# Graph network kernel: layer 0 multiplies h by the neighbour weights before it takes neighbour means

## The reference

```python
h = relu(layernorm(x))
mask = (adj > 0)
deg = sum(mask, axis=1)
agg = mask @ h / max(deg, 1)
self_f = h @ W_self + b_self
nb_f = agg @ W_nb + b_nb
x = x + relu(concatenate([self_f, nb_f]) @ W_comb + b_comb)
h = relu(layernorm(x))
# layer 1: five steps of a gated propagation with adj and adj.T, then two dense layers
x = x + layer1(h, adj)
```

## Time and profile before

| | us |
|---|---|
| median of 3 runs | 1231.34 (1231.26 to 1233.05) |
| profiled execution, its own time | 1229.56 |
| its span, first to last instruction | 1227.8 |
| TensorE busy | 1218.7 (99%) |
| VectorE busy | 757.1 (62%) |
| ScalarE busy | 287.8 (23%) |

### The profile page before, as it was taken

How to read it: one execution, slowest core, us unless ns; L and a number is a source line. 1 busy time by engine, 2 the same in 40 slices (tenths; PEclk the granted TensorE clock), 3 DMA queues, 4 the chain that set the end, 5 groups by cost and what they waited for, 6 DMA issues and landing times.

```text
span 1227.8 us, 12867 instructions
## 1 busy us (share of the span) xinstructions
PE 1218.7 (99%) x4872; PEld 589.9 (48%) x4872; DVE 757.1 (62%) x1264; ACT 287.8 (23%) x568; POOL 15.4 (1%) x15
## 2 busy tenths in 40 slices
PE   8999999999999999999999999999999999999998
PEld 5766644444444444444444444444444444444445
DVE  6677735787984474487367339626725864662674
ACT  5766100022321121033012113301202230120121
POOL 4000000000000000000000000000000000000000
PEclk9999999999999999999999999999999999999999
DMA  9545734960019505800830660191084039015202
GB/s 330 172 155 172 291 138 172 315 240 0 1 34 341 207 0 179 300 1 35 311 135 0 243 236 1 57 352 71 3 307 169 1 141 336 2 69 206 90 1 69
DMA packets 44506, 180.61 MB, mean 147 GB/s; under 512 B 3489, under 2 KB 13474, under 8 KB 29346
## 3 DMA queue, kind: packets, MB, share of 16 engines
q1 hardware_dynamic: 43440, 176.04, 39.5%
q0 software_dynamic: 720, 3.67, 0.8%
q10 hardware_dynamic: 290, 0.14, 0.0%
HBM read 144.71 MB, written 35.13 MB: 146 GB/s over the span
## 4 chain that ended last, share of the span: by engine, by line
PE 93%; DVE 4%; DMA 1%; issue 1%; ACT 1%; SPq 0%; DVEq 0%
PE bank L352 90%; PE bank L418 1%; PE bank L520 1%; DMA SN<-in_x 1%; PE bank L439 0%; ACT A L770 0%; PE bank L470 0%; DVE LF L1203 0%; PE bank L380 0%; DVE stat L993 0%; DVE GR L1350 0%; DVE first_GZ L1350 0%; DVE first_GH L1323 0%; DVE first_GZ L1353 0%; DVE GR L1353 0%
## 5 line engine op out<-in xcount | busy, mean ns | idle before, releaser
L352 PE MATMUL bank<-slot,LF 128*128 128x512 f16 x1792 | 389.4, 379 | 0.0
L352 PEld LDWEIGHTS bank<-slot,LF 128*128 128x128 f16 x1792 | 175.3, 98 | 210.1 <-issue 2.3
L352 PE MATMUL bank<-X,W 128*128 128x512 f32 x384 | 180.5, 592 | 0.0
L352 PE MATMUL bank<-XT,W 128*128 128x512 f32 x288 | 135.3, 592 | 0.0
L352 PEld LDWEIGHTS bank<-X,W 128*128 128x128 f32 x384 | 72.5, 190 | 88.0 <-issue 86.9
L352 PE MATMUL bank<-AT,SN 128*128 (+1 forms) x256 | 97.0, 379 | 0.0
L352 PE MATMUL bank<-A,SN 128*128 (+1 forms) x256 | 97.0, 379 | 0.0
L1249 DVE TENSOR_TENSOR u_buf<-bank,m_buf 128x512 f32<-128x512 f32 x16 | 11.1, 692 | 134.0 <-PE bank L352 134.0
L352 PEld LDWEIGHTS bank<-XT,W 128*128 128x128 f32 x288 | 54.7, 190 | 68.9 <-issue 68.2
L770 ACT ACTIVATE m_buf<-bank 128x512 f32<-128x512 f32 x46 | 27.4, 595 | 231.9 <-PE bank L352 231.9
L352 PE MATMUL bank<-DR,work 128*128 128x512 f16 x256 | 65.6, 379 | 0.4 <-DVE DR L1064 0.2
(11 more groups left out here) (217 smaller groups left out, 1420.9 us busy)
## 6 DMA issues: line engine op xcount, KB each, us to landing
slot<-quad_d SPq DMA_DIRECT2D x112, 1024.0 KB, 4.9
WG<-in_adj SPq DMA_DIRECT2D x32, 512.0 KB, 4.4
quad_d<-AT SPq DMA_DIRECT2D x12, 1024.0 KB, 5.0
quad_d<-A SPq DMA_DIRECT2D x12, 1024.0 KB, 8.6
quad_d<-spare SPq DMA_DIRECT2D x4, 1024.0 KB, 4.0
SN<-in_x SPq DMA_DIRECT2D x2, 1024.0 KB, 10.3
x_d<-SN POOLq DMA_DIRECT2D x4, 512.0 KB, 4.2
x1o<-x_d SPq DMA_DIRECT2D x1, 2048.0 KB, 8.1
```

The source lines that it names most:

```text
L352: return pe.matmul(o, l, r, start=start, stop=stop, skip_group_check=again)
```

## The change

Since a mean over neighbours and a product with weights can be exchanged, h is multiplied by the neighbour slices of `W12` first (`values`), and the neighbour sums run over these values. `hi_lo` now holds two fp16 parts of the values and a column of ones. In `mean_sum` the mask tiles are stationary and the values move (256 columns, and 257 with the ones, which gives the degree), so sums come out with nodes on partitions, one tile in each of banks 0 to 3. The neighbour weights are scaled by a norm computed in the front (`w2_norm`). Own products (`own_term`) are made in bank 7 while a block's sums still run, DVE keeps them with the bias (`keep_own`), and `sums` combines straight from the banks. `values`, `turn_h`, `turn_h2` and `own_term` share bank 7. In the front, loads are cut and reordered, weight products and bias row come first, and values of the first quarter and the turns of two quarters are made before the loop; the 12 bias columns go one by one into the first 12 steps. At the end, the last two output tiles are added and stored singly, one of them issued by ACT.

```diff
-STAGE_AT = [8, 13, 14]
-H2_BANKS = [6, 6, 6, 4]
-H2_AT = 12
+STAGE_AT = [7, 12, 13]
 ACT_MOVES = [i for i in range(NT * NB) if i % 2 == 0 or (i >= NT and i % NT in (3, 11))]
-HIGH_AT = [1, 4, 8]
-LOW_AT = [2, 5, 9]
-TURN_AT = [4, 7, 10, 12]
+G_AT = {0: (1, 0), 1: (1, 1), 4: (2, 0), 5: (2, 1), 8: (3, 0), 9: (3, 1)}
+T_AT = {2: (2, 0), 3: (2, 1), 6: (3, 0), 7: (3, 1)}
+H2_AT = (10, 12)
+OWN_AT = 14
+COLUMNS = 300
...
+        hi_lo = at("hi_lo", 144 * KB, [P, NT, 2 * D + 2], FP16)
...
+        term = [own0[:, 0, :], own0[:, 1, :], h2[:, 2, :], h2[:, 3, :]]
...
+        low_banks = ctx.enter_context(nc.psum_tensor("low_banks", [P, 4, 512], FP32))
+        bank = [low_banks[:, i, :] for i in range(4)]
+        bank += [ctx.enter_context(nc.psum_tensor(f"bank{i}", [P, 512], FP32)) for i in range(4, 8)]
...
+        def value_bank(q, a):
+            return bank[4 + a] if q == 0 else bank[7]
...
+            sp.dma_start(wgR[0][:, 0, :], wg_t[0:P, :]).then_inc(ld_wj[0], 16)
+            sp.dma_start(ioR[:, 0, 0, :], w_in[0:P, :]).then_inc(ld_wj[0], 16)
+            x_quarter(0)
+            x_quarter(1)
+            sp.dma_start(wgR[0][:, 1, :], wg_t[P:2 * P, :]).then_inc(ld_wj[1], 16)
+            sp.dma_start(ioR[:, 0, 1, :], w_in[P:2 * P, :]).then_inc(ld_wj[1], 16)
+            sp.dma_start(wgR[1][:, 0, :], wg_t[2 * P:3 * P, :]).then_inc(ld_wo[0], 16)
+            sp.dma_start(ioR[:, 1, 0, :], w_out[0:P, :]).then_inc(ld_wo[0], 16)
+            x_quarter(2)
+            x_quarter(3)
+            sp.dma_start(wgR[1][:, 1, :], wg_t[3 * P:4 * P, :]).then_inc(ld_wo[1], 16)
+            sp.dma_start(ioR[:, 1, 1, :], w_out[P:2 * P, :]).then_inc(ld_wo[1], 16)
...
+            sp.wait_ge(o2_dve, 2 * NB - 1)
+            sp.dma_start(out_v[:, NT - 4:NT - 2, :], res[:, NT - 4:NT - 2, :]).then_inc(st_out, 16)
+            sp.wait_ge(o2_dve, 2 * NB + 1)
+            sp.dma_start(out_v[:, NT - 1, :], res[:, NT - 1, :]).then_inc(st_out, 16)
+            sp.wait_ge(st_out, 16 * (NB + 1))
+            sp.wait_ge(st_last, 16)
...
+            def turn_h(q, f):
+                pe.wait_ge(h_ready, q + 1)
+                if q == 0:
+                    pe.wait_ge(w12_out, 2)
+                if q == 1 and f == 0:
+                    pe.wait_ge(hT_act, 1)
+                if q == 1 and f == 1:
+                    pe.wait_ge(hT_dve, 1)
+                if q >= 2 and f == 0:
+                    pe.wait_ge(g_lo, 2 * q)
+                if q >= 2 and f == 1:
+                    pe.wait_ge(hT_act, q + 1)
+                o = bank[6 + f] if q < 2 else bank[7]
+                for t in range(BT):
+                    last = pe.transpose(o[:, t * P:t * P + P], h32[:, BT * q + t, f * P:f * P + P], ident)
+                last.then_inc(hT_ready, 1)
+            def values(q, a):
+                pe.wait_ge(hT_act, q + 1)
+                pe.wait_ge(hT_dve, q + 1)
+                pe.wait_ge(w2_ready, 1)
+                if q == 0 and a == 1:
+                    pe.wait_ge(bias_out, 1)
+                if q >= 1 and a == 1:
+                    pe.wait_ge(g_lo, 2 * q + 1)
+                o = bank[4 + a] if q == 0 else bank[7]
+                for e in range(2):
+                    n0 = q * BN + (2 * a + e) * P
+                    for f in range(FT):
+                        last = mm(o[:, e * D:e * D + D], ST[:, f, n0:n0 + P], W12[:, 2 + f, :], f == 0, f == 1)
+                last.then_inc(g_ready, 1)
...
+            for j in range(2):
+                pe.wait_ge(ld_wj[j], 32)
+                fuse(0, j)
+                fuse(1, j)
+                if j == 0:
+                    pe.wait_ge(w2_square, 1)
+                    mm(bank[4][:, 0:1], one_col, norm[:, 0:1], True, True).then_inc(w2_norm, 1)
+            turn_h(0, 0)
+            turn_h(0, 1)
+            pe.wait_ge(ld_wo[0], 32)
+            pe.wait_ge(fused_out, 2)
+            fuse(2, 0)
+            pe.wait_ge(fused_out, 4)
+            fuse(3, 0)
+            values(0, 0)
+            values(0, 1)
+            pe.wait_ge(ld_wo[1], 32)
+            fuse(2, 1)
+            fuse(3, 1)
+            turn_h(1, 0)
+            turn_h(1, 1)
...
+                for q in range(BT):
+                    if m == 0 and b > 0:
+                        pe.wait_ge(agg_read, BT * (b - 1) + q + 1)
+                    l = mk[:, q * P:q * P + P]
+                    if m == 0:
+                        mm(bank[q][:, 0:D + 1], l, hi_lo[:, m, D:2 * D + 1], True, False, True)
+                    last = mm(bank[q][:, 0:D], l, hi_lo[:, m, 0:D], False, False, True)
+                    if m > 0:
+                        last = mm(bank[q][:, 0:D + 1], l, hi_lo[:, m, D:2 * D + 1], False, m == NT - 1, True)
+                last.then_inc(mask_used, 1)
...
+            def own_term(b, half):
+                pe.wait_ge(hT_act, b + 1)
+                pe.wait_ge(hT_dve, b + 1)
+                if b == 0 and half == 0:
+                    pe.wait_ge(g_lo, 8)
+                elif b > 0 and half == 1:
+                    pe.wait_ge(s_dve, b)
+                else:
+                    pe.wait_ge(own_kept, 2 * b + half)
+                for e in range(2):
+                    n0 = b * BN + (2 * half + e) * P
                     for f in range(FT):
-                        mm(bank[f][:, :], hi_lo[:, m, s, f * P:f * P + P], mk, m == 0 and s == 0,
-                           m == NT - 1 and s == 1)
+                        last = mm(bank[7][:, e * D:e * D + D], ST[:, f, n0:n0 + P], W12[:, f, :], f == 0, f == 1)
+                last.then_inc(own_made, 1)
...
+                if i < 12:
+                    bias_column(i)
+                if i in G_AT:
+                    values(*G_AT[i])
+                if i in T_AT:
+                    turn_h(*T_AT[i])
+                if b > 0 and m in H2_AT:
+                    turn_h2(b - 1, H2_AT.index(m))
+                if i == 11:
+                    own_term(0, 0)
+                if m == OWN_AT:
+                    own_term(b, 1)
                 if i + LEAD < NT * NB:
                     turn_adj(i + LEAD)
-                if i % NT == NT - 1:
-                    dense(i // NT, 0)
-                if i % NT == 1 and i > NT:
-                    dense(i // NT - 1, 1)
+                if m == NT - 1 and b + 1 < NB:
+                    own_term(b + 1, 0)
...
-            pe.wait_ge(agg_act, NB)
-            pe.wait_ge(agg_dve, NB)
-            pe.wait_ge(rdeg_ready, NB)
+            pe.wait_ge(agg_read, BT * NB)
...
-            dense(NB - 1, 1)
...
+            fused(0)
+            fused(1)
+            move_h(0)
+            convert(0, 0)
+            convert(0, 1)
+            high(0, 0)
+            convert(1, 0)
+            high(0, 1)
+            convert(1, 1)
+            act.wait_ge(var_ready, 2)
+            nc.scalar.activation(nrm[:, 1, 8:16], nrm[:, 0, 8:16], ACT.Sqrt).then_inc(sqrt_ready, 1)
+            fused(2)
+            fused(3)
+            move_h(1)
...
+            def low(q, a):
+                dve.wait_ge(g_hi, 2 * q + a + 1)
+                t = BT * q + 2 * a
+                v.tensor_tensor(hi_lo[:, t:t + 2, D:2 * D], value_bank(q, a)[:, :].rearrange("p (e d) -> p e d", e=2),
+                                hi_lo[:, t:t + 2, 0:D], ALU.subtract).then_inc(g_lo, 1)
...
+            dve.wait_ge(w2_norm, 1)
+            v.tensor_scalar(norm[:, 1:2], bank[4][:, 0:1], 1e-30, None, ALU.max).then_inc(w2_norm, 1)
+            variance(range(0, 8), 0)
+            dve.wait_ge(bias_made, 1)
+            v.tensor_copy(bias0, bank[5][:, 0:D]).then_inc(bias_out, 1)
+            newton(0, 8, 1)
             normal(0)
+            dve.wait_ge(w2_root, 1)
+            link(v.reciprocal(norm[:, 0:1], norm[:, 2:3]))
+            link(v.tensor_scalar(norm[:, 3:4], norm[:, 0:1], SCALE, None, ALU.mult))
+            v.tensor_scalar(w2, w2, norm[:, 3:4], None, ALU.mult).then_inc(w2_ready, 1)
+            turned_h(0)
             normal(1)
-            low(0)
+            dve.wait_ge(ld_x[2], 16)
+            row_stats(range(8, 12), 0)
+            low(0, 0)
+            dve.wait_ge(ld_x[3], 16)
+            row_stats(range(12, 16), 0)
+            low(0, 1)
+            variance(range(8, 16), 0)
+            turned_h(1)
+            newton(8, 16, 2)
+            normal(2)
...
+            def keep_own(b, half):
+                dve.wait_ge(own_made, 2 * b + half + 1)
+                dve.wait_ge(bias_out, 1)
+                if b > 0 and half == 1:
+                    dve.wait_ge(sn_hi, b)
+                for e in range(2):
+                    ins = v.tensor_tensor(term[2 * half + e], bank[7][:, e * D:e * D + D], bias0, ALU.add)
+                ins.then_inc(own_kept, 1)
...
+                link(v.tensor_scalar(rdeg[:, tiles], low_banks[:, :, D], 1.0, norm[:, 3:4], ALU.max, ALU.mult))
                 link(v.reciprocal(rdeg[:, tiles], rdeg[:, tiles]))
+                dve.wait_ge(own_kept, 2 * b + 2)
+                if b == 0:
```

(56 more changed lines are left out.)

336 lines of the change are left out of this document (131 added, 205 removed).

## The result

The changed kernel takes 1239.57 us (median; 1236.59 to 1244.95) against 1231.31 (1230.72 to 1233.05) on the same chip. The ratio is 1.0067, 95% interval 1.0054 to 1.0079: 8.3 us slower, where 2.9 were forecast, and outside the range. Its profiled execution took 1240.02 (span 1238.2), 10.4 more than that of before.

| us | before | after | difference | forecast |
|---|---|---|---|---|
| start to first neighbour sum | 27.67 | 39.40 | +11.7 | +5.1 |
| loop, to where spreading begins (before: its effective end) | 111.3 | 111.5 | +0.2 | -0.8 |
| spreading to the last matmul's end (before without the 3.46 of dense) | 1084.7 | 1084.7 | 0 | 0 |
| from there to the end | 4.1 | 2.6 | -1.5 | -1.4 |

The account below looks back on a forecast made before the run. TensorE was taken to bound the kernel, with 93% of the chain that ends last. Front +5.1, loop -0.8 and tail -1.4 gave +2.9 on 1231.3, so 1234.2 us; range 1226.5 to 1238.0.

Parts of the forecast that it names:

- Part 1: TensorE's work: one-column matmuls go, 512-column ones become twice as many of 256 or 257; net -5.7 us.
- Part 2: Front before the loop: first neighbour sum at 32.8 us against 27.67, so +5.1.
- Rival D: Before the first neighbour sum, 28.4 to 32.8: clock falls to 1.2 GHz, costing 2.2 us; total 1236.4, chance 10%.
- Part 3: Block 0, from first neighbour sum to node tile 14's transposes: 36.3 us, including 1.35 of stalls for the values' bank.
- Part 4: Blocks 1 to 3: TensorE stalls 1.9 us a block for VectorE's chain; block period 23.8 us.
- Rival B: Blocks 1 to 3: VectorE keeps up, stalls stay 0.6 us a block, period 22.5; total 1230.3, chance 22%.
- Part 5: End of the loop: TensorE stalls 2.3 us ahead of spreading; loop 110.5 us against 111.3.
- Part 6: Tail: smaller last addition and last transfer; -1.4 us, bounds 0 and -2.
- bound of +6.5 for the front: Front before the loop: upper bound on its added time, in us, if the weights land 1 us later.

Follow-up runs that it names:

- six mendings: Changed kernel with fusions reordered, GpSimd's second group held, 13 warm-up matmuls, two more ScalarE moves, ScalarE/VectorE front steps reordered, spreading bank by bank: 1228.69 us, ratio 0.9980.
- the changed order: Changed kernel with the first half of the output weights' fusions ahead of the first turn of h: 1237.48 us, ratio 1.0051.

## Why the prediction was right or wrong

**Part 1, TensorE's work: right.** A tile of sums alone takes 0.885 us (80.97 to 81.86), 0.874 were worked out from the straight line; over 64 tiles that is 0.7 us. An operation of 256 columns costs 0.885 / 8 = 111 ns, not 109, and the doubled number of weight loads cost nothing that shows. The net saving was 5.0 instead of 5.7.

**Part 2, the front: wrong, and it is nearly the whole miss.** First sum at 39.40 against 32.8; term by term:

| step of the walk | forecast | measured | miss |
|---|---|---|---|
| first product starts | 6.14 | 6.93 | +0.8 |
| weight products and bias row | 5.96 | 7.61 | +1.65 |
| fusions and norm | 2.83 | 2.83 | 0 |
| norm's end to the first turn | 3.92 | 6.42 | +2.5 |
| to the end of the second turn | 10.45 | 12.09 | +1.6 |
| to the first neighbour sum | 3.5 | 3.52 | 0 |

- *First product.* "The same 1 MB stands ahead, so I keep 6.14": here it was 6.93, in the profiles of its variants 6.57 to 6.87. No run took this term apart.
- *Weight products.* Their durations were taken from a stretch where TensorE had been at work for long. Here the first 3 us ran at half speed, and 24 records took 7.05 (7.18 and 7.20 in two other profiled executions with 10 warm-up matmuls, 5.42 to 5.44 in three more of them; 5.42 in all three with 13).
- *Norm to h.* The mis-sized term is the 1.38 for four normalised tiles. The row was right for its place, where GpSimd was idle, and the change moved the work to another place, beside GpSimd. It measured 3.28, 1.9 of the 2.5; the rest lies in the small steps ahead of it (0.54 for 0.17, 0.36 for 0.17). The prediction summed GpSimd's store and never asked what GpSimd's arithmetic did to VectorE. That the mechanism is this one is shown by taking it away (1.38 with GpSimd elsewhere, and the chain at 3.96) and by moving it (3.44 where GpSimd then was).
- *Fusions, values, turns.* TensorE ran at 1.2 GHz for 3.4 microseconds. Rival D had the right mechanism and the right size (2.2 for 1.6), but a chance of 10% and a place where nothing fell: the wait of 1.54 before the first sum left the clock at 1.00. The real cause was the wait of 3.59 that the step before had grown. The two are one chain: a late h makes a long wait, and a long wait makes slow products.

**Part 3, block 0: right in kind.** From the first sum to the point in tile 14 it took 36.96 (39.40 to 76.36), 36.3 forecast; the stalls for the values' bank were five of 0.28, as worked out.

**Part 4, blocks 1 to 3: right.** 23.9 against 23.8 (23.90 and 23.91). The own term waited 0.44 (0.55 forecast). The stall of 1.3 forecast ahead of tile 26 came in pieces: 0.30 ahead of tile 21, 0.06 ahead of 24, 0.68 ahead of 25 (the row at 90.87; its transposes began at 89.97 and cost 0.22) and 0.13 ahead of 26, together 1.2. (The terms that the prediction lists for VectorE add up to 10.04, which puts mask 26 at 15.44 and the stall at 1.1; it wrote 15.65 and 1.3.) The move given to ScalarE showed that it is VectorE's chain. Rival B's 22.5 was not reached even by the kernel with six mendings (23.06).

**Part 5: right.** Gap 2.23 against 2.3. The loop's 111.5 against 110.5 is block 0's 0.7 and 0.1 a block. **Part 6: right.** -1.5 against -1.4; alone, on the kernel before, -1.6 and -1.9.

So five parts of six held, and the sum fell with the one that has the fewest repetitions and the most engines in it. The range failed with it: its bound of +6.5 for the front took a late load in, but no contention, and D stood in it as a single term of 2.2 when it had to be added to whatever made TensorE wait. The trace of before held the start times that would have shown the collision (the forecast put VectorE's normalisation, begun at 20.64 before, ahead of 18.85, and GpSimd was at work there until 18.84 already before), and in the casts at 6.14 and 6.40 a price for it.

## What to carry to other kernels

When a change moves work to another time, write down for each moved row which other engines were busy beside it where it was measured, and which will be where it goes; a duration holds for its neighbourhood only. Look in the trace for one instruction that appears with and without such a neighbour; here it stood at 6.14 and 6.40. A wait of TensorE as long as those behind which the clock fell here (2.08 us and more) is to be priced twice, with the wait and, as a chance, with 1.6 us or more that the half clock costs behind it; work pulled into it, or its cause shortened, mends both. And mend a front as a whole: of the front's single edits the split of GpSimd's work gained 3.7 us, the warm-up (1.6) and the changed order (2.1) stayed within the noise, and all six mendings together gained 10.9. Only then was the change faster than what it replaced, and even then not clearly faster than its changed end alone. Last, read the granted clock of every execution beside its time, or a fall of the clock passes for an effect of the edit.

## What the runs showed of the hardware

- **GpSimd makes part of VectorE's instructions wait.** Four tensor-scalar operations of 256 fp32 columns from SBUF to SBUF take 1.38 us beside an idle GpSimd, and 2.30 (twice), 3.28, 3.29, 3.44 and 3.91 beside a busy one. This is no even slowing. Those that began together with GpSimd's addition of two tensors took 1.97 (four cases), one that began 1.0 us into it 0.98, and each of them ended 0.15 to 0.16 us behind it; beside GpSimd's tensor-scalar operation single ones took from 0.40, as alone, to 1.06. One of 8 columns went from 0.17 to 0.54, 0.76, 0.81 and 1.58, a cast of 128 columns from 0.23 to 0.85. Statistics were not slowed (0.35 to 0.37 each with and without), nor operations that read PSUM (512 columns 0.69 in both cases). GpSimd lost little: two of its tensor-scalar operations took 4.38 or 4.39 in most profiled executions, in the changed kernel too, and 4.42 to 4.58 in four. The Trainium skill ("GPSIMD Engine Reference", section Key points) says that GpSimd shares its SBUF interfaces with VectorE, and that instructions which use two ports or have two inputs in SBUF contend. The trace agrees in that one with two inputs in SBUF was hit (8 columns, 0.36 for 0.17) and those that read PSUM were not; that the normalisation is one that uses two ports is not shown here.
- **The clock falls within a kernel.** It fell to 1.2 GHz during idle times of 4.35 and 4.47 us, shortly behind those of 2.08, 2.40 and 3.59, and stayed up behind waits of 0.83 to 1.54. A wait of 2.08 us or more does not always bring it down: behind the gap of 2.23 ahead of spreading it fell in three profiled executions (to 1.2 GHz at 147.0, 149.7 and 151.3) and stayed at 1.00 in five. It cost 1.6 us in the changed kernel, and more in the kernel with GpSimd held back, where it stood at 0.50 from 34 to 40. The warning of the Trainium skill that the prediction cited ("TensorE: Matmul & The Clock Gate", section Why this matters for your kernels) is thus borne out here, which no row of before had shown.
- **The start has two speeds.** The 24 records behind the warm-up took 5.4 or 7.05 to 7.20 us, with pauses of 1.03 to 1.29 ahead of the slow kind and 0.17 to 1.47 ahead of the fast, so the pause doesn't decide it by itself. In the three slow executions the records start 0.43 us apart up to about 10.2 and 0.22 apart behind it; in the fast ones they are 0.22 apart from the second on. With 13 warm-up matmuls all three were fast; that is few, and why one execution reaches full speed earlier than another stays open.
